# Moving 24 of 170 scatter columns from a graph kernel's first stage into its layers

## The chip, the core and the metric

The kernel runs on one core of one Trainium2 chip. A core has five engines with a queue each, which run in order and meet only at semaphores: TensorE (PE, matrix products), VectorE (DVE), ScalarE (ACT), GpSimd (POOL) and SyncE (SP, which mostly issues DMAs). The metric is device time in microseconds (us), the median of several runs; one execution was recorded by the profiler.

## What is computed

Three layers of a graph network over 1250 nodes of width 512 and 21,250 edges, then a residual norm, then a network over the edges with four attributes per edge, then the nodes again. Cut to what matters:

```
# first network, L = 3 layers
for l in range(3):
    neigh = segment_sum(h[src], dst) * inv_deg
    h = h @ Ws_self[l] + neigh @ Ws_neigh[l] + bs[l]      # relu but for the last
x = layernorm(x + h)
# second network
e     = mlp(edge_attr_4)                                   # 21250 x 4 -> 512
e_new = mlp([e, mesh_nfeat[src], x[dst]]) + e
agg   = segment_sum(e_new, dst)
x     = layernorm(x + mlp([x, agg]) + x)
```

## The kernel before

The edges are sorted by destination into 176 tiles of 128 edges, in ten buckets of 125 destination nodes each. The program has these stages.

*First stage* (`phase_a`). VectorE sorts and computes for each edge its slot. GpSimd writes the sorted index pairs to DRAM with 72 indirect DMAs (lines 400 and 404). An indirect DMA on GpSimd takes one column of up to 125 edges and sends each to the row that a table names; GpSimd generates its descriptors. The edge attributes, four floats per edge, go the same way into `s_attrs`, 170 columns (`EC`), one DMA each, by `scatter_attr` (line 145). `row_i` holds the rows, `k_attrs` the attributes. 24 of the columns (`ATTR_EARLY`) are issued in the first stage behind the pairs. Meanwhile TensorE makes weight products and the first layer's products. Last comes the *edge count*: for each tile VectorE makes two one-hot matrices (`hot_src`, line 605, and `hot_dst`, line 606), and TensorE multiplies them (lines 851 and 854) and adds them up into a table of edge counts by node pair, in three banks of PSUM. Four tiles are in flight; after four written out ones the loops run four tiles a pass. At the end of a bucket ScalarE copies the banks out. So that no tile is added before the copy of the bucket before, TensorE waits for a gate per tile and bank. SyncE opens the even tiles' gates and GpSimd the odd ones', both with the loop in `open_gates` (lines 272 to 277), which GpSimd reaches behind its 24 columns. The gates wait for `copied_out`, which TensorE starts at line 859.

*Graph layers* (`phase_b`). In each layer TensorE adds up the neighbours of ten groups of 125 nodes with the count table (lines 1226 and 1227, 20 matmuls a group, two groups ahead), VectorE mixes each sum with the node's own part (`b_mixed`, line 1052) and splits the table for the next (`b_a_lo`, line 1045), and then TensorE makes the next products (lines 73 to 75). GpSimd meanwhile issues `scatter(0, 130)`: the next 130 attribute columns, in batches of 17 (`BACKLOG`) with a semaphore for every second batch. Only in the third layer does somebody wait for GpSimd: VectorE's `normalise` handles two groups at a time, adds `x` (line 1060), takes mean and variance (lines 1063 to 1070), and GpSimd raises the variance to the power -1/2 (line 1015), which VectorE needs at line 1073. After every second power GpSimd issues four of the last 16 columns (`ATTR_LATE`), and after the last it loads the attributes back in slot order (line 1022).

*Edges and nodes* (`phase_c`, `phase_d`). About 1500 us of work on the edge tiles, where TensorE is nearly always busy, and then the nodes. GpSimd builds the operand from the attributes and gathers node rows.

Of the kernel before, what the change touches and what calls it, by code (L numbers as in the profile page):

```python
# [43 lines left out]
EP, EC = 125, E // 125  # L44
# [9 lines left out]
HALF_TILES = TILES // 2  # L54
PAD = P - 1
BACKLOG = 17
ATTR_EARLY, ATTR_LATE, ATTR_PAIR = 24, 16, 4
RECIP_BITS = 20
RECIP = (1 << RECIP_BITS) // NPB + 1
assert all(n * RECIP >> RECIP_BITS == n // NPB for n in range(N)) and N * RECIP < 1 << 24  # L60
# [77 lines left out]
def batched(columns, u):  # L138

    return sum(c // BACKLOG % 2 == u for c in range(columns))  # L140


def scatter_attr(pool, scratch, k, c):

    return pool.indirect_dma_start(scratch["attrs"], bass.IndirectOffsetOnAxis(ap=k["row_i"][0:EP, c:c + 1], axis=0),  # L145
                                   k["attrs"][0:EP, A4 * c:A4 * (c + 1)], None)
# [12 lines left out]
def phase_a(nc, ctx, t, scratch, keep):  # L159
# [9 lines left out]
    def sem(name):  # L169
        semaphores.append(nc.alloc_semaphore("a_" + name))  # L170
        return semaphores[-1]
# [60 lines left out]
    k, src_t, dst_t = keep, keep["src_t"], keep["dst_t"]  # L232
# [10 lines left out]
    count_bank, degree_bank = (bank[0], bank[1], bank[6]), bank[7]  # L243
    pairs_ok, attr_rows_ok = sem("pairs_ok"), sem("attr_rows_ok")
    scattered = [sem(f"scattered{i}") for i in range(2)]
    attr_scattered = [sem(f"attr_scattered{i}") for i in range(2)]
    pairs_in, pairs_read, pairs_turned = sem("pairs_in"), sem("pairs_read"), sem("pairs_turned")
    next_in = sem("next_in")
    centred, turned, turned_out, gains_ok, bias_mm, cols_ok = (
# [19 lines left out]
    def open_gates(engine, u):  # L269


        engine.wait_ge(tables_ok, 1)
        with engine.Fori(0, TILES // 2) as i:
            bucket1 = engine.value_load(k["tile_bucket1"][0:1, ds(2 * i + u, 1)], min_val=1, max_val=NB)
            for b in range(3):
                engine.wait_ge(copied_out[b], bucket1)
                engine.sem_inc(gate[b][u], 1)
# [8 lines left out]
    def rows_stored(u, upto):  # L286

        return 16 * (NJ // 2) + 16 * sum(len(names) for names, _, _ in vectors[u:upto:2])
# [83 lines left out]
    @block.gpsimd  # L372
    def _(pool):
        pool.iota(dst_grid[:], [[1, P]], base=0, channel_multiplier=0).then_inc(pool_const, 1)
        pool.iota(src_grid[:], [[NPB, NB], [1, P]], base=0, channel_multiplier=0).then_inc(pool_const, 1)
        pool.iota(tile_no[:], [[1, TILES + 1]], base=0, channel_multiplier=0,
                  allow_small_or_imprecise_dtypes=True).then_inc(pool_const, 1)
        pool.iota(k["grid"][:], [[1, P]], base=0, channel_multiplier=0,
                  allow_small_or_imprecise_dtypes=True).then_inc(pool_const, 1)
        pool.iota(place[:], [[-1, EC]], base=(1 << PLACE_BITS) - 1, channel_multiplier=0).then_inc(pool_const, 1)  # L380
        pool.iota(aside[:], [[1, EC]], base=SLOTS, channel_multiplier=ASIDE,
                  allow_small_or_imprecise_dtypes=True).then_inc(pool_const, 1)
        for i in range(2):
            pool.memset(jobs_out[i][:], 0.0).then_inc(pool_const, 1)
        pool.wait_ge(dve_const, 2)

        pool.affine_select(out=k["ident"][:], in_=k["ident"][:], compare_op=ALU.not_equal, fill=1.0, base=0,
                           pattern=[[-1, P]], channel_multiplier=1).then_inc(pool_const, 1)
        pool.affine_select(out=before[:], in_=before[:], compare_op=ALU.is_gt, fill=0.0, base=0,
                           pattern=[[1, P]], channel_multiplier=-1).then_inc(pool_const, 1)  # L390

        pool.wait_ge(pads_out, 32)
        pool.wait_ge(pairs_ok, 1)
        singles = scratch["pairs"].rearrange("a (b c) -> (a b) c", c=1)
        for c in range(CHUNKS + REST):
            u = c // BACKLOG % 2
            if c % BACKLOG == 0 and c >= 2 * BACKLOG:
                pool.wait_ge(scattered[u], 16 * batched(c, u))
            if c < CHUNKS:
                pool.indirect_dma_start(scratch["pairs"], bass.IndirectOffsetOnAxis(ap=chunk_row[:, c:c + 1], axis=0),  # L400
                                        sort_pay[:, CHUNK * c:CHUNK * (c + 1)].bitcast(F32), None).then_inc(scattered[u], 16)
            else:
                j, at = c - CHUNKS, c - CHUNKS + EC - REST
                pool.indirect_dma_start(singles, bass.IndirectOffsetOnAxis(ap=rest_row[:, j:j + 1], axis=0),
                                        sort_pay[:, at:at + 1].bitcast(F32), None).then_inc(scattered[u], 16)
        pool.wait_ge(attrs_in, 16)
        pool.wait_ge(attr_rows_ok, 1)
        for c in range(ATTR_EARLY):
            scatter_attr(pool, scratch, k, c).then_inc(attr_scattered[c // BACKLOG % 2], 16)
        open_gates(pool, 1)  # L410
        for u in range(2):
            pool.wait_ge(attr_scattered[u], 16 * batched(ATTR_EARLY, u))

    @block.vector
    def _(dve):
# [487 lines left out]
def phase_b(nc, ctx, t, scratch, keep):  # L903
# [9 lines left out]
    def sem(name):  # L913
        return ctx.enter_context(nc.semaphore("b_" + name))
# [3 lines left out]
    k = keep  # L918
# [27 lines left out]
    attr_scattered, attrs_in = [sem(f"attr_scattered{i}") for i in range(2)], sem("attrs_in")  # L946
# [19 lines left out]
    @block.sync  # L966
    def _(sp):
        for r in range(1, LAYERS):
            sp.wait_ge(w_split, 2 * r)
            for i in range(2):  # L970
                sp.dma_start(w[i][:], chunked(products[r][i])).then_inc(w_in, 16)
            sp.wait_ge(self_ok, NB * r)
            if r < LAST:
                sp.dma_start(bias[0][:], rows(t["L0_gnn_bs"][r + 1]).broadcast_to([P, D])).then_inc(bias_in, 16)
        sp.dma_start(bias[0][:], rows(t["L1_gnn_node_b0"]).broadcast_to([P, D])).then_inc(bias_in, 16)
        sp.dma_start(bias[1][:], rows(t["L1_gnn_edge_b0"]).broadcast_to([P, D])).then_inc(bias_in, 16)
        sp.dma_start(bias2[:], rows(scratch["edge_shift"]).broadcast_to([P, D])).then_inc(bias_in, 16)

        def load(i):
            if i >= X_BUFS:  # L980
                sp.wait_ge(res_ok, i - X_BUFS + 1)
            move_rows(sp, x[i % X_BUFS][:], node_rows(t["x"], node(LAST, i)), x_in[i % X_BUFS])

        for i in range(NB):
            load(i)
        edges.sync_first(sp)
        for i in range(NB):
            sp.wait_ge(u_lo_ok, NB * LAST + i + 1)
            u = i % OUT_BUFS
            if i < HEAD:  # L990
                move_rows(sp, node_rows(scratch["dst_head"], i), out[u][:, 1, :], head_stored[i])
            move_rows(sp, node_rows(scratch["node_own"], i), out[u][:, 0, :], stored[u])
            move_rows(sp, node_rows(scratch["dst_table"], i), out[u][:, 1, :], stored[u])
            edges.sync_early(sp, i)
        for i in range(NB):
            move_rows(sp, node_rows(scratch["x1"], i), h[:, i, :], x1_stored)
        for u in range(OUT_BUFS):
            sp.wait_ge(stored[u], 2 * MOVED * len(range(u, NB, OUT_BUFS)))
        edges.sync(sp)

    @block.gpsimd
    def _(pool):
        def scatter(first, end):
            for c in range(first, end):
                u = c // BACKLOG % 2
                if c % BACKLOG == 0 and c >= 2 * BACKLOG:
                    pool.wait_ge(attr_scattered[u], 16 * batched(c, u))
                scatter_attr(pool, scratch, k, ATTR_EARLY + c).then_inc(attr_scattered[u], 16)

        columns = EC - ATTR_EARLY  # L1010
        scatter(0, columns - ATTR_LATE)
        for i in range(NB):
            pool.wait_ge(var_ok, i + 1)
            pool.sem_inc(tick, 1)
            pool.tensor_tensor(dev[i % 2][:, 1:2], dev[i % 2][:, 0:1], k["half"][0:NPB, :], ALU.pow).then_inc(dev_ok, 1)
            left = ATTR_LATE - ATTR_PAIR * (i // 2)
            if i % 2 and left > 0:
                scatter(columns - left, columns - left + ATTR_PAIR)
                if left == ATTR_PAIR:
                    for u in range(2):  # L1020
                        pool.wait_ge(attr_scattered[u], 16 * batched(columns, u))
                    pool.dma_start(k["attrs"][:], scratch["attrs"].rearrange("(p t) a -> p (t a)", p=P)).then_inc(attrs_in, 16)
        pool.wait_ge(attrs_in, 16)
        edges.gpsimd(pool)
# [1236 lines left out]
```

## Time and profile before

| | us |
|---|---|
| median of 3 runs | 2257.26 |
| lowest and highest | 2256.71, 2258.75 |
| the profiled execution's own time | 2256.75 |
| its span in the trace | 2255.0 |
| first stage, to the start of the layers | 324 |
| graph layers | 324 to about 640 |

Busy over the span: TensorE 97%, VectorE 67%, ScalarE 54%, GpSimd 54%. A timeline row gives the start, the duration, the engine, the line, the operation with output and inputs, a count where equal neighbours are merged, and in brackets the idle time of the engine before it with what ended it. "POOLq" and the like are the sequencers of the engines, which read the queue, wait and branch ahead of the engine proper.

### The profile page before, as it was taken

The numbers are of one execution on the slowest core, as the hardware profiler recorded it, in microseconds if no ns is written. First come the engines' busy times: TensorE is split into PE (matmuls) and PEld (weight loads), VectorE is DVE, ScalarE is ACT, GpSimd is POOL, SyncE is SP. The second block draws the span as 40 slices with busy tenths as digits, with TensorE's granted clock in tenths as the row PEclk, the third lists the DMA queues.
The fourth block names the chain that finished last, engine by engine and source line by source line (L and its number), as shares of the span: only waits on it lengthen the run. The fifth ranks groups of instructions, "written<-read, shape, count | busy, mean of one in ns | idle before, by whom it ended". The sixth has DMA issues, their size and how long they took to land. (4 is left out here: it accounts for less than half of the span.)

```text
span 2255.0 us, 44895 instructions
## 1 busy us (share of the span) xinstructions
PE 2190.3 (97%) x13039; PEld 1881.9 (83%) x13040; DVE 1502.7 (67%) x3372; ACT 1218.0 (54%) x2244; POOL 1206.8 (54%) x1721
## 2 busy tenths in 40 slices
PE   7999989999999999999999999999999999999898
PEld 4367888888789989899898998989989989889776
DVE  8425975344756777767767667766776676767666
ACT  2221114333256676677666767667667667667421
POOL 0775028885535555565555555555555555555223
PEclk9999999999999999999999999999999999999899
DMA  6421001112363333323332333333323332333131
GB/s 203 127 56 41 0 6 40 8 40 54 114 210 88 64 62 63 62 60 65 60 65 61 65 60 65 63 63 60 65 60 60 65 65 61 60 65 65 27 92 44
DMA packets 81814, 149.81 MB, mean 66 GB/s; under 512 B 20523, under 2 KB 20989, under 8 KB 81754
## 3 DMA queue, kind: packets, MB, share of 16 engines
q0 software_dynamic: 47248, 93.38, 21.5%
q1 hardware_dynamic: 34505, 55.67, 7.8%
q8 instruction: 33, 0.54, 0.1%
q14 instruction: 28, 0.22, 0.0%
HBM read 128.90 MB, written 19.71 MB: 66 GB/s over the span
## 5 line engine op out<-in xcount | busy, mean ns | idle before, releaser
L1667 ACT ACTIVATE b_bank<-c_bias 128x512 f32<-128x512 f32 x528 | 316.4, 599 | 15.1 <-PE b_bank L1779 10.0
L145 POOL DMA_INDIRECT s_attrs<-k_attrs,k_row_i x170 | 224.4, 1320 | 168.0 <-POOLq L2233 117.2
L1600 DVE CUSTOM_DVE_ANT_0 b_bank<-b_bank,c_p,k_floor 128x512 f32<-128x512 f32 x176 | 132.5, 753 | 255.5 <-PE b_bank L1801 254.6
L1445 POOL DMA_INDIRECT c_from_src<-s_dst_table,c_at_nodes x173 | 278.5, 1610 | 32.2 <-issue 32.2
L1856 PE MATMUL b_bank<-k_m_hi,c_pt_hi 128*128 128x512 f32 x704 | 293.8, 417 | 0.0
L1432 POOL DMA_INDIRECT c_from_src<-s_mesh_table,c_at_nodes x176 | 202.3, 1149 | 152.3 <-POOL c_at_nodes L1428 142.5
L1857 PE MATMUL b_bank<-k_m_lo,c_pt_hi 128*128 128x512 f32 x704 | 277.9, 395 | 0.0
L1451 POOL TENSOR_TENSOR c_dev<-c_var,k_half 128x1 f32<-128x1 f32 x176 | 99.3, 564 | 327.5 <-DVE c_var L1582 327.5
L1858 PE MATMUL b_bank<-k_m_hi,c_pt_lo 128*128 128x512 f32 x704 | 273.9, 389 | 0.0
L1738 ACT ACTIVATE c_h<-c_from_src 128x512 f32<-128x512 f32 x176 | 111.3, 632 | 263.4 <-DVE c_from_src L1621 263.4
L1799 PE MATMUL b_bank<-c_m_hi,c_ht_hi 128*128 128x384 f32 x704 | 222.5, 316 | 6.3 <-DVE c_ht_lo L1587 6.0
L1799 PE MATMUL b_bank<-k_m_hi,c_pt_hi 128*128 128x384 f32 x704 | 224.7, 319 | 0.0
L1801 PE MATMUL b_bank<-c_m_hi,c_ht_lo 128*128 128x384 f32 x704 | 218.6, 311 | 0.0
L1800 PE MATMUL b_bank<-c_m_lo,c_ht_hi 128*128 128x384 f32 x704 | 217.7, 309 | 0.0
L1801 PE MATMUL b_bank<-k_m_hi,c_pt_lo 128*128 128x384 f32 x704 | 217.1, 308 | 0.0
L1800 PE MATMUL b_bank<-k_m_lo,c_pt_hi 128*128 128x384 f32 x704 | 216.9, 308 | 0.0
L1616 DVE SCALAR_TENSOR_TENSOR c_rp_lo<-c_p,c_dev,c_rp_hi 128x512 fp32r<-128x512 f32 x176 | 132.3, 751 | 74.0 <-ACT c_rp_hi L1730 73.8
L1858 PEld LDWEIGHTS b_bank<-k_m_hi,c_pt_lo 128*128 128x128 f32 x704 | 132.8, 189 | 32.4
L1730 ACT ACTIVATE c_rp_hi<-c_p,c_dev 128x512 fp32r<-128x512 f32 x176 | 127.7, 726 | 54.9 <-POOL c_dev L1467 54.9
L1663 ACT ACTIVATE c_p<-b_bank 128x512 f32<-128x512 f32 x176 | 105.6, 600 | 92.3 <-PE b_bank L1776 91.7
L1467 POOL TENSOR_TENSOR c_dev<-c_var,k_half 128x1 f32<-128x1 f32 x176 | 133.0, 756 | 40.5 <-DVE c_var L1603 35.9
L1856 PEld LDWEIGHTS b_bank<-k_m_hi,c_pt_hi 128*128 128x128 f32 x704 | 132.4, 188 | 23.9
(352 smaller groups left out, 5859.9 us busy)
## 6 DMA issues: line engine op xcount, KB each, us to landing
c_from_src<-s_mesh_table,c_at_nodes POOLq DMA_INDIRECT x176
c_from_src<-s_dst_table,c_at_nodes POOLq DMA_INDIRECT x173, 4.7
s_attrs<-k_attrs,k_row_i POOLq DMA_INDIRECT x170
a_mesh<-in_L_gnn_mesh_nfeat_dram SPq DMA_DIRECT2D x10, 224.0 KB
k_h<-in_x_dram SPq DMA_DIRECT2D x10, 224.0 KB
s_mesh_table<-a_mesh_out SPq DMA_DIRECT2D x10, 224.0 KB
b_x<-in_x_dram SPq DMA_DIRECT2D x10, 224.0 KB
s_node_own<-b_out SPq DMA_DIRECT2D x10, 224.0 KB
```

The lines of the kernel that those rows point to most:

```text
L145: return pool.indirect_dma_start(scratch["attrs"], bass.IndirectOffsetOnAxis(ap=k["row_i"][0:EP, c:c + 1], axis=0), k["attrs"][0:EP, A4 * ...
L1432: pool.indirect_dma_start(from_src[u][:], None, scratch["mesh_table"], bass.IndirectOffsetOnAxis(ap=at_nodes[u][:, 0:1], axis=0)).then_inc ...
L1445: pool.indirect_dma_start(from_src[u][:], None, scratch["dst_head" if head else "dst_table"], bass.IndirectOffsetOnAxis(ap=at_nodes[u][:, ...
L1467: pool.tensor_tensor(dev[u][:, 0:1], var[u][:, 2:3], k["half"][:], ALU.pow).then_inc(dev1_ok, 1)
L1600: dve.tensor_tensor_reduce(var1_bank[:], var1_bank[:], p[u % 2][:], 1.0 / D, k["floor"][:, 0:1], ALU.mult, ALU.add, var[u][:, 0:1]).then_i ...
L1667: act.activation(bank[:], bias[:, m, :], ACT.Copy).then_inc(bank_set, 1)
L1799: pe.matmul(to, left[0][:, c, :], high, start=False, stop=False, skip_group_check=True)
L1800: pe.matmul(to, left[0][:, c, :], low, start=False, stop=False, skip_group_check=True)
L1801: last = pe.matmul(to, left[1][:, c, :], high, start=False, stop=(c == KC - 1), skip_group_check=True)
L1856: pe.matmul(edge_bank[:], left[0], m_hi[1][:, c, :], start=False, stop=False, skip_group_check=True)
L1857: pe.matmul(edge_bank[:], left[0], m_lo[1][:, c, :], start=False, stop=False, skip_group_check=True)
L1858: last = pe.matmul(edge_bank[:], left[1], m_hi[1][:, c, :], start=False, stop=(c == KC - 1), skip_group_check=True)
```

## The change

The constant for the early columns is gone. All 154 columns that were not among the last 16 are issued at the start of the layers, where 130 were; the first stage issues none. The wait for the 24 at the end of the first stage and its two semaphores go too, and the semaphores of the layers count from column 0.

```diff
-ATTR_EARLY, ATTR_LATE, ATTR_PAIR = 24, 16, 4
+ATTR_LATE, ATTR_PAIR = 16, 4
...
         pool.wait_ge(attrs_in, 16)
         pool.wait_ge(attr_rows_ok, 1)
-        for c in range(ATTR_EARLY):
-            scatter_attr(pool, scratch, k, c).then_inc(attr_scattered[c // BACKLOG % 2], 16)
         open_gates(pool, 1)
-        for u in range(2):
-            pool.wait_ge(attr_scattered[u], 16 * batched(ATTR_EARLY, u))
...
-                scatter_attr(pool, scratch, k, ATTR_EARLY + c).then_inc(attr_scattered[u], 16)
-
-        columns = EC - ATTR_EARLY
-        scatter(0, columns - ATTR_LATE)
+                scatter_attr(pool, scratch, k, c).then_inc(attr_scattered[u], 16)
+
+        scatter(0, EC - ATTR_LATE)
         for i in range(NB):
...
             if i % 2 and left > 0:
-                scatter(columns - left, columns - left + ATTR_PAIR)
+                scatter(EC - left, EC - left + ATTR_PAIR)
```

GpSimd's queue at the end of the first stage, before: the last pair DMAs, the 24 attribute columns, the gate loop (the table's entry is loaded at L274), the end of the stage, and the first instruction of the layers.

```order
18 L404 DMA s_pairs<-a_sort_pay,a_rest_row 44700x1 x30
19 L145 DMA s_attrs<-k_attrs,k_row_i 22528x4 x24
20 L273 UNCONDITIONAL_BRANCH
21 L273 ISA
22 L274 TENSOR_LOAD k_tile_bucket
23 L274 ISA x2
24 L273 REGISTER_ALU
25 L273 COMPARE_AND_BRANCH
```

The same place after the change (line numbers are up to six lower):

```order
18 L403 DMA s_pairs<-a_sort_pay,a_rest_row 44700x1 x30
19 L272 UNCONDITIONAL_BRANCH
20 L272 ISA
21 L273 TENSOR_LOAD k_tile_bucket
22 L273 ISA x2
23 L272 REGISTER_ALU
24 L272 COMPARE_AND_BRANCH
```

The gate loop now stands directly behind the pairs.

GpSimd's queue from the start of the layers to the second pair of powers, before:

```order
28 L1001 UNCONDITIONAL_BRANCH
29 L145 DMA s_attrs<-k_attrs,k_row_i 22528x4 x130
30 L1015 TENSOR_TENSOR b_dev_2164<-b_dev_2164,k_half 125x1
31 L1015 TENSOR_TENSOR b_dev_2165<-b_dev_2165,k_half 125x1
32 L145 DMA s_attrs<-k_attrs,k_row_i 22528x4 x4
```

The same place after it:

```order
27 L996 UNCONDITIONAL_BRANCH
28 L145 DMA s_attrs<-k_attrs,k_row_i 22528x4 x154
29 L1009 TENSOR_TENSOR b_dev_2138<-b_dev_2138,k_half 125x1
30 L1009 TENSOR_TENSOR b_dev_2139<-b_dev_2139,k_half 125x1
31 L145 DMA s_attrs<-k_attrs,k_row_i 22528x4 x4
```

24 more columns stand ahead of the first two powers; the groups of four behind them are as before. The queues of the other engines keep their order.

## Rows read from the trace of the kernel before

**Rows 1.** Timeline of GpSimd, first and last early column, first column of the layers.
```profile
171.83 1.19 POOL L145 DMA_INDIRECT s_attrs<-k_attrs,k_row_i  x1 [0.30 <-issue]
...
206.17 1.18 POOL L145 DMA_INDIRECT s_attrs<-k_attrs,k_row_i  x1 [0.30 <-issue]
...
324.53 1.19 POOL L145 DMA_INDIRECT s_attrs<-k_attrs,k_row_i  x1 [117.17 <-POOLq L2233]
```

**Rows 2.** Stretches: length, busy us (instructions) per engine, granted clock, DMA share, GB/s.
```profile
195.00:200.00 5.00, 5.00 (x49) 3.86 (x48) 3.24 (x8) 0.60 (x1) 4.00 (x4) 1.00 0.09 5
200.00:205.00 5.00, 2.31 (x25) 1.39 (x22) 1.09 (x3) 0.00 (x0) 3.87 (x4) 0.94 0.09 4
205.00:210.00 5.00, 3.21 (x26) 2.40 (x27) 2.71 (x9) 0.00 (x0) 2.05 (x2) 0.50 0.07 2
```

**Rows 3.** Timeline of VectorE, one-hot tiles in the loop's first passes.
```profile
200.17 0.57 DVE L605 TENSOR_SCALAR a_hot_src<-a_src_grid,k_src_t 128x1280 bf16<-128x1280 int16 x1 [1.32 <-PE a_bank L854]
...
204.65 0.57 DVE L605 TENSOR_SCALAR a_hot_src<-a_src_grid,k_src_t 128x1280 bf16<-128x1280 int16 x1 [3.75 <-remote]
...
207.66 0.55 DVE L605 TENSOR_SCALAR a_hot_src<-a_src_grid,k_src_t 128x1280 bf16<-128x1280 int16 x1 [2.29 <-remote]
...
208.30 0.55 DVE L605 TENSOR_SCALAR a_hot_src<-a_src_grid,k_src_t 128x1280 bf16<-128x1280 int16 x1
...
211.05 0.55 DVE L605 TENSOR_SCALAR a_hot_src<-a_src_grid,k_src_t 128x1280 bf16<-128x1280 int16 x1 [0.17 <-PE a_bank L854]
```

**Rows 4.** Timeline of TensorE, count matmuls of tile 0 and of tile 4.
```profile
198.76 0.17 PE L854 MATMUL a_bank<-a_ones,a_hot_dst 128*128 128x2 bf16 x1
...
202.28 0.23 PE L851 MATMUL a_bank<-a_hot_dst,a_hot_src 128*128 128x128 bf16 x1 [0.45 <-issue]
202.99 0.27 PE L851 MATMUL a_bank<-a_hot_dst,a_hot_src 128*128 128x128 bf16 x2 [0.48 <-issue]
```

**Rows 5.** Sequencers by line: count, ns min/median/max, first and last start us.
```profile
L273 POOLq MOVE  x1: 29/29/29, 189.5 to 189.5; - x1
...
L859 PEldq EVENT_SEMAPHORE  x3: 51/51/51, 194.7 to 195.0; - x3
...
L274 POOLq SEQ_ASSERT  x1: 590/590/590, 205.3 to 205.3; - x1
```

**Rows 6.** Timeline of GpSimd, last column before the powers, first and second powers.
```profile
532.80 1.19 POOL L145 DMA_INDIRECT s_attrs<-k_attrs,k_row_i  x1 [0.30 <-issue]
553.72 1.20 POOL L1015 TENSOR_TENSOR b_dev<-b_dev,k_half 125x1 f32<-125x1 f32 x2 [19.73 <-DVE b_dev L1070]
...
564.78 1.19 POOL L1015 TENSOR_TENSOR b_dev<-b_dev,k_half 125x1 f32<-125x1 f32 x2 [1.89 <-DVE b_dev L1070]
```

**Rows 7.** Timeline in the second layer, a column of GpSimd and VectorE beside it.
```profile
439.47 2.19 POOL L145 DMA_INDIRECT s_attrs<-k_attrs,k_row_i  x1 [0.30 <-issue]
...
439.11 1.48 DVE L1045 TENSOR_TENSOR b_a_lo<-k_adj,b_a_hi 125x1280 fp32r<-125x1280 int16 x1
```

**Rows 8.** Timeline of VectorE in the third layer, around the first pair.
```profile
550.68 1.28 DVE L1060 TENSOR_TENSOR b_mixed<-b_mixed,b_x 125x512 f32<-125x512 f32 x2
...
554.33 1.18 DVE L1073 TENSOR_SCALAR k_h<-b_mixed,b_moments,b_dev 125x512 f32<-125x512 f32 x2 [0.65 <-POOL b_dev L1015]
555.43 0.74 DVE L1052 SCALAR_TENSOR_TENSOR b_mixed<-b_bank,b_inv_degree,k_h 125x512 f32<-125x512 f32 x1
```

**Rows 9.** Stretches, columns as in rows 2, in the third layer.
```profile
555.00:560.00 5.00, 5.00 (x24) 4.14 (x23) 5.00 (x5) 2.32 (x2) 4.34 (x3) 1.00 0.05 1
```

**Rows 10.** Timeline of TensorE, first matmul of the seventh sum (sum 6).
```profile
567.36 0.47 PE L1226 MATMUL b_bank<-b_u_hi,b_a_hi 125*128 125x512 f32 x1 [0.65 <-DVE b_mixed L1052]
```

**Rows 11.** Timeline of TensorE, large matmuls after its idle time at 320.
```profile
325.08 0.80 PE L1226 MATMUL b_bank<-b_u_hi,b_a_hi 125*128 125x512 f32 x1 [4.55 <-ACT b_a_hi L1153]
...
330.75 0.40 PE L1226 MATMUL b_bank<-b_u_hi,b_a_hi 125*128 125x512 f32 x1
330.98 0.40 PE L1227 MATMUL b_bank<-b_u_lo,b_a_hi 125*128 125x512 f32 x1
```

**Rows 12.** Timeline of VectorE, the last pair.
```profile
595.41 1.16 DVE L1073 TENSOR_SCALAR k_h<-b_mixed,b_moments,b_dev 125x512 f32<-125x512 f32 x2 [2.15 <-POOL b_dev L1015]
```

More of the change, by code:

```diff
@@ L245, in phase_a @@
     scattered = [sem(f"scattered{i}") for i in range(2)]
-    attr_scattered = [sem(f"attr_scattered{i}") for i in range(2)]
     pairs_in, pairs_read, pairs_turned = sem("pairs_in"), sem("pairs_read"), sem("pairs_turned")
@@ L1017, in _ @@
             if i % 2 and left > 0:
-                scatter(columns - left, columns - left + ATTR_PAIR)
+                scatter(EC - left, EC - left + ATTR_PAIR)
                 if left == ATTR_PAIR:
                     for u in range(2):
-                        pool.wait_ge(attr_scattered[u], 16 * batched(columns, u))
+                        pool.wait_ge(attr_scattered[u], 16 * batched(EC, u))
                     pool.dma_start(k["attrs"][:], scratch["attrs"].rearrange("(p t) a -> p (t a)", p=P)).then_inc(attrs_in, 16)
```

## The prediction

> **What bounds the kernel now.** The change only moves GpSimd's descriptor work, so I read GpSimd's own timeline first, then whoever waits at the two places from which and to which the work moves. [Rows 1] is GpSimd's timeline: the 24 early columns start at 171.83 us and the last at 206.17, one every 1.49 us (34.34 / 23), each 1.19 busy and 0.30 idle. Then GpSimd issues nothing more until the graph layers start at 324.53.
>
> The first place is the edge count, which begins at about 198 us. The table by stretches [rows 2] shows TensorE 5.00 of 5.00 us busy until 200, then 2.31 and 3.21 of 5.00, and the granted clock at 0.50 in the second of these. VectorE's timeline [rows 3] says how much is lost: it makes the one-hot tiles, and from 207.66 to 208.30 it makes one in 0.64 us, the pace that it keeps to the end of the count. But the first tiles of its loop start at 200.17, 204.65, 207.66 and 208.30, after idle times of 1.32, 3.75 and 2.29 us, the last two put down to nothing that the profile can name ("remote"). TensorE trickles in the same way: two matmuls, then 0.45 to 0.48 us of "issue" [rows 4]. The gates are not the cause: GpSimd's sequencer had entered the gate loop at 189.5, ahead of its own queued columns, and the gates were held only by TensorE's start signal at 194.7; yet that sequencer too shows a register check of 590 ns at 205.3 [rows 5]. All sequencers slow together, the pieces come one every 0.71 to 0.76 us, half of GpSimd's 1.49, and it ends at 207.4, when the last early column ends (206.17 + 1.18). I read it as contention between the descriptor work of the columns and four engines that all issue small instructions at their highest rate; the trace shows the coincidence and not the mechanism.
>
> The second place is the last graph layer. GpSimd's timeline [rows 6]: the 130th layer column starts at 532.80 and ends at 533.99, and then GpSimd waits 19.73 us for the first variances (b_dev, line 1070), which arrive at 553.72. That is all the room there is: 553.72 - 534.29 = 19.4 us before the first power on line 1015 is late.
>
> **What the change does, part by part.**
>
> *Out of the first stage: 24 columns, 24 x 1.49 = 35.8 us of GpSimd and 24 scatters.* GpSimd was not waited for there directly. What goes is the overlap with the start of the count. Three tiles after 200.17 at 0.64 is 202.1; the same tile started at 208.30 [rows 3]: 6.2 us. The 1.32 us before 200.17 would mostly go as well (tile 0 had been counted by 198.93 [rows 4]), up to 0.9, and the 0.17 and similar idle times near 211, which follow from the clock at 0.50, up to 0.5. So the gain is 6.2 to 7.6 if my reading is right and 0 if it is wrong; I take **-7.0**. It passes on whole, since the rest of the count runs at VectorE's pace and what follows starts when the count has ended. The waits for the scatter's semaphores at the stage's end go too, at nothing: those scatters had landed 110 us earlier.
>
> *Into the layers: the same 24 columns ahead of the first power.* They stand in GpSimd's queue before line 1015, and nothing can overtake them. In the old clock of the layers (all of it moves by the gain above), columns 131 to 154 start at 534.29 and, at 1.49 each, end at 570.1. Some are dearer: a column that starts while VectorE runs a two-input operation waits for that operation's end. The one at 439.47 took 2.19 us instead of 1.19 while a_lo ran from 439.11 to 440.59 [rows 7], so it was held 1.0. Between 540 and 552 there are three a_lo of 1.48 us and the two adds of the first pair, the last of them in [rows 8]; laying the columns on them one after another gives 0.4 + 1.0 + 1.3, with some rounding 2.4 us. Bounds: 0 (no column meets one) and 5.6 (three times 1.48 and 1.2 in full). So GpSimd comes free at 572.5, against 553.72: the first pair's power is **18.8 us late** (16.4 to 21).
>
> The Trainium skill ("SBUF — State Buffer", section "Who interferes with whom") infers that a tensor_tensor does not hold up descriptor generation. The row at 439.47 speaks against it here; by the page the 2.4 would be 0, the lateness 16.4 and the total 2.4 lower.
>
> *What of the 18.8 reaches the end.* VectorE waits at line 1073 for that power (0.65 us now), and everything behind it on VectorE is in order: the two normalised tiles, the next mix at 555.43, the next a_lo [rows 8]. From 555 to 560 VectorE is busy 5.00 of 5.00 us [rows 9], and it is so to 593.3 (595.41 - 2.15 [rows 12]) except 0.6 us for each power and small gaps: it has no slack in which to catch up. TensorE has hardly any either: it runs two sums ahead and already waits 0.65 us for b_mixed at 567.36 [rows 10]; so it passes the delay on whole. It would stand still for some 17 us from 557.5 and restart at a low clock. After the 4.55 us gap at 325.08 it ran at half speed till 330.75: 12 of the large matmuls at 0.43 us instead of 0.23 [rows 11], 2.5 us lost. Here that is hidden: sum 4 would end at 556.1 + 18.8 + 4.5 + 2.5 = 581.9, and VectorE asks for it only at 566.47 + 18.8 = 585.3. If this cover were gone it would cost 2.5; I take 0. The waits that follow keep their size: GpSimd has four late columns between two powers as before, and the 2.15 us before 595.41 [rows 12] hangs on GpSimd's own chain, which is shifted like the rest. The reload of the attributes behind the last column moves along with it, with no new waiter. From 601 on TensorE has the lead again, and the edges run as before. So **+18.8**.
>
> *Small things.* GpSimd's queue is 24 entries longer in one place and shorter in another; SyncE's queue is unchanged. The removed semaphores and the renumbered batches cost nothing: the first batch wait in the layers comes 34 columns in, when 17 have long landed.
>
> **Sum.** 2256.75 (the profiled run's own time; its span is 2255.0) - 7.0 + 18.8 = 2268.55. The median of the runs shown is 2257.26, 0.5 above, which is within their spread; I state **2268.8**.
>
> **Rivals.**
> 1. *The count starts no sooner.* The stall at 200 to 208 belongs to something else that stays, such as the first pass through the loops' code. For it: it starts as VectorE and TensorE enter their loops at 200, and later bucket ends have no such stall. Against: GpSimd's sequencer had been in its loop since 189.5 and stalls as well, the half-period of 0.74 us is GpSimd's, and the stall ends with the last column. Gain 0: 2256.75 + 18.8 = 2275.6. The Trainium skill ("Runtime: NRT & Kernel Launch", "Instruction fetch mechanics") says that a taken branch outside the pages at hand forces a fetch before execution goes on. By that rule the stall would stay, which is this rival; VectorE's long idle times however stand inside the straight code of one pass, which speaks against it.
> 2. *The lateness costs more than itself.* GpSimd stays behind after the first pair, since the late columns meet other VectorE operations, or the low clock is not covered. Each group of four has little slack (GpSimd waited 1.89 us before the power at 564.78 [rows 6]); if a group takes 1 us more than its slack, or the 2.5 us of clock shows, the sum is 3 to 6 higher: 2272 to 2275.
> 3. *Faster than before.* The lateness is absorbed in the last layer, because TensorE and VectorE there have work that can go ahead of line 1073, so only the gain is left: 2256.75 - 7.0 = 2249.8. It decides once less than 7 of the 18.8 us gets through. Against it: VectorE's queue is in order, it has nothing but that wait, and TensorE already waits for it at 567.36 [rows 10]. Even columns at 1.19 without the idle 0.30 would be late by 8.9 (534.0 + 24 x 1.19 - 553.72).
>
> **How the numbers follow.** Chances: the forecast 0.74 (its own range 2265 to 2271.5: gain 6.2 to 7.6, lateness 16.4 to 21), rival 1 0.13, rival 2 0.08, rival 3 0.05. The likeliest is the forecast, 2268.8. To hold 8 times in 10 the range must take in part of rivals 1 and 2: 2265 to 2276. A measurement of this kernel can tell about 0.2% (4.5 us) from no change. Faster by more than that: 0.04; within: 0.04 (a mostly absorbed delay); slower: 0.92.
>
> **What would show it.** Right: VectorE's loop tiles follow each other at 0.64 us from 200 on and the granted clock stays at 1.00 there; the layers start at about 317.5 instead of 324.5; the first power follows directly on a column, at about 565.5 on the new clock; VectorE idles about 19 us before line 1073 once, and TensorE about 17 before a sum; later waits are as before. Rival 1: the same idle times of 3.75 and 2.29 at the loop's start. Rival 2: longer VectorE waits for the second to fourth powers. Rival 3: no long VectorE idle time at line 1073. The forecast would be wrong above all if columns ran at another pace than 1.49 us in the stretch from 534 on.

## The result and the profile after

The changed kernel took 2268.88 us (median of 5 runs, 2264.41 to 2271.16) against 2257.26 before (5 runs, 2256.71 to 2258.75). The ratio is 1.0041, with a 95% interval from 1.0029 to 1.0052: slower by 6.5 to 11.7 us. (The ratio isn't the quotient of the two medians, which lie 11.6 us apart, at the upper end of that interval.) The profiled execution was the shortest of the five, 2264.41 us, with a span of 2262.7.

**The first place.** Stretches of the kernel after, columns as in [rows 2]:

```profile
200.00:205.00 5.00, 5.00 (x97) 5.00 (x95) 4.99 (x17) 0.00 (x0) 0.00 (x0) 1.00 0.00 2
205.00:210.00 5.00, 4.50 (x79) 4.10 (x77) 5.00 (x17) 1.43 (x4) 0.00 (x0) 1.00 0.00 0
```

VectorE's timeline after, the first tiles of its loop:

```profile
199.50 0.55 DVE L600 TENSOR_SCALAR a_hot_src<-a_src_grid,k_src_t 128x1280 bf16<-128x1280 int16 x1 [0.25 <-PE a_bank L849]
200.23 0.55 DVE L600 TENSOR_SCALAR a_hot_src<-a_src_grid,k_src_t 128x1280 bf16<-128x1280 int16 x1
200.86 0.55 DVE L600 TENSOR_SCALAR a_hot_src<-a_src_grid,k_src_t 128x1280 bf16<-128x1280 int16 x1
```

TensorE does 97 matmuls in the stretch from 200, where it did 25 [rows 2]; the granted clock stays at 1.00; the tiles come every 0.63 us; and the waits of 1.32, 3.75 and 2.29 us [rows 3] are one of 0.25 us. GpSimd's timeline after, from the last pair to the layers, and at the end of the long row of columns:

```profile
170.81 1.19 POOL L403 DMA_INDIRECT s_pairs<-a_sort_pay,a_rest_row  x1 [0.30 <-issue]
317.28 1.18 POOL L145 DMA_INDIRECT s_attrs<-k_attrs,k_row_i  x1 [145.28 <-POOLq L2227]
...
561.75 1.18 POOL L145 DMA_INDIRECT s_attrs<-k_attrs,k_row_i  x1 [0.30 <-issue]
562.95 1.21 POOL L1009 TENSOR_TENSOR b_dev<-b_dev,k_half 125x1 f32<-125x1 f32 x2
...
574.02 1.19 POOL L1009 TENSOR_TENSOR b_dev<-b_dev,k_half 125x1 f32<-125x1 f32 x2 [1.90 <-DVE b_dev L1064]
```

The layers start at 317.28 instead of 324.53. The wait of 19.73 us before the first power [rows 6] is gone; the power stands directly behind a column. The second power has its wait of 1.90 us, as before.

**The second place.** VectorE's timeline after: the instruction for the first pair's variances, the first pair, the last pair.

```profile
545.12 0.27 DVE L1064 TENSOR_SCALAR b_dev<-b_moments 125x1 f32<-125x1 f32 x2
563.59 1.16 DVE L1067 TENSOR_SCALAR k_h<-b_mixed,b_moments,b_dev 125x512 f32<-125x512 f32 x2 [18.20 <-POOL b_dev L1009]
...
605.01 1.16 DVE L1067 TENSOR_SCALAR k_h<-b_mixed,b_moments,b_dev 125x512 f32<-125x512 f32 x2 [2.51 <-POOL b_dev L1009]
```

TensorE's timeline and the stretches around it:

```profile
565.55 0.76 PE L1220 MATMUL b_bank<-b_u_hi,b_a_hi 125*128 125x512 f32 x1 [16.20 <-DVE b_mixed L1046]
...
570.38 0.40 PE L1221 MATMUL b_bank<-b_u_lo,b_a_hi 125*128 125x512 f32 x1
```
```profile
555.00:560.00 5.00, 0.00 (x0) 0.00 (x0) 0.00 (x0) 0.00 (x0) 4.04 (x4) 0.50 0.08 2
...
565.00:570.00 5.00, 4.45 (x11) 3.51 (x12) 5.00 (x5) 3.07 (x2) 4.39 (x3) 0.50 0.05 1
570.00:575.00 5.00, 5.00 (x23) 4.09 (x22) 4.30 (x10) 1.28 (x1) 2.80 (x4) 0.96 0.37 104
```

From 555 to 560 TensorE, VectorE and ScalarE do nothing and GpSimd issues columns. VectorE waits 18.20 us where it waited 0.65 [rows 8], and TensorE 16.20 us. TensorE then runs at half speed till 570.4, while VectorE beside it is busy 5.00 of 5.00 us, so this low clock is hidden: the second power comes 11.07 us after the first (574.02 - 562.95), against 11.06 before.

**Where the time went.** Measured from marks in the two traces:

| piece, us | before | after | difference |
|---|---|---|---|
| first tile of VectorE's count loop at | 200.17 | 199.50 | -0.67 |
| from it to the layers' first column | 124.36 | 117.78 | -6.58 |
| from there to the first power | 229.19 | 245.67 | +16.48 |
| the rest of the span | 1701.28 | 1699.75 | -1.53 |
| span | 2255.0 | 2262.7 | +7.7 |

The third row is the lateness, the second the gain. The first and the last differ from run to run of the same kernel: a second trace of the changed kernel (below) starts its loop at 202.33 and spans 2266.9.

### The profile page after: what moved, and what is told of

It reads as the page before. It is cut to its first block and busy times, and to the rows that moved or that the text cites. A ratio compares the mean times of both kernels' runs of the same rounds, so it can differ in the third digit from the quotient of the medians.

```text
span 2262.7 us, 44890 instructions
## 1 busy us (share of the span) xinstructions
PE 2186.2 (97%) x13036; PEld 1879.4 (83%) x13040; DVE 1501.2 (66%) x3372; ACT 1218.3 (54%) x2244; POOL 1209.3 (53%) x1721
```

## The experiments

Theory A, the one on record: columns issued on GpSimd at the start of the edge count slow all engines there while they last (cost about 7), and 24 more columns ahead of the first power make it late by about 18.8, which passes on whole. Rivals: the slow start has another cause that stays; the layers' end absorbs part; GpSimd's delay grows behind the first pair. The kernels of each of the four rounds ran on one chip beside the kernel before.

**The changed kernel again**, on the chip of the next three.

> The changed kernel once more, for a second profile and for its spread: its runs lay between 2264.4 and 2271.2, those of before within 2 us. Forecast: median about 2268.5; the layers start at 317 and VectorE waits 18.2 us in each profile, so that what differs between runs lies later or in the clock.

Measured: 2268.64 us against 2258.12, ratio 1.0053 (1.0039 to 1.0067). Its distances are 117.78 from the loop's first tile to the layers and 245.68 from there to the first power, within 0.01 of the first trace. So both terms repeat, and what varies is the start of the count and the part behind the layers. The layers start at 320.11 in this trace, not at the expected 317, because the count starts 2.8 us later.

**The 24 columns left out altogether.** The kernel leaves out part of the attribute table, so its result is not that of the task; the time shows the gain without the price.

```diff
+ATTR_LATE, ATTR_PAIR = 16, 4          # none early
...
-        scatter(0, columns - ATTR_LATE)
+        scatter(0, EC - ATTR_LATE - 24)
```

> The changed kernel with 24 of its 170 attribute columns left out, those of the layers just ahead of the last 16: the first stage is as in the changed kernel, the layers have 130 columns ahead of the first power as before the change. Only the gain is left. Forecast (contention of the columns with the start of the edge count): 2257.3 - 7.0 = 2250.3, layers start at about 317, VectorE waits 0.6 us for the first power. Rival 1 (the stall belongs to the loops' first pass): 2257 and layers at 324.

Measured: 2251.81 us, ratio 0.9970 (0.9959 to 0.9981), that is -6.8 us (-9.3 to -4.3). The distance from loop to layers is 117.76, and GpSimd waits for the first variances again (the layers start at 321.30, not at 317, since the loop's first tile comes as late as 203.54):

```profile
549.50 1.20 POOL L1009 TENSOR_TENSOR b_dev<-b_dev,k_half 125x1 f32<-125x1 f32 x2 [18.25 <-DVE b_dev L1064]
```

**The 24 columns twice**: early as before, and once more ahead of the first power.

```diff
+        for c in range(24):
+            scatter_attr(pool, scratch, k, c).then_inc(repeated, 16)
         for i in range(NB):
```

> The kernel before, with the 24 early columns issued a second time in the layers behind the 130, ahead of the first power (the same values to the same rows). Only the lateness is left. Forecast: GpSimd is free 18 to 19 us late and all of it reaches the end: 2257.3 + 18.8 = 2276, layers start at 324.5. If part of the lateness were absorbed downstream: under 2272. If the low clock after TensorE's idle time showed as well: about 2278.

Measured: 2274.46 us, ratio 1.0073 (1.0060 to 1.0087), +16.5 us (13.5 to 19.6). VectorE's timeline of this kernel shows the stall of the first place and the wait of the second, side by side:

```profile
206.38 0.76 DVE L605 TENSOR_SCALAR a_hot_src<-a_src_grid,k_src_t 128x1280 bf16<-128x1280 int16 x1 [3.58 <-remote]
...
572.71 1.17 DVE L1076 TENSOR_SCALAR k_h<-b_mixed,b_moments,b_dev 125x512 f32<-125x512 f32 x2 [16.72 <-POOL b_dev L1017]
```

The first power comes 245.67 us after the layers' start, as in the changed kernel. The two halves add up: -6.8 + 16.5 = +9.7, between the 9.3 and the 12.0 that the two ratios of the changed kernel give. Within intervals this wide, no absorption and no growth. The traces say it more sharply. From the first power to the end, the four kernels in which that power is late (the changed one twice, this one, and the one with eight early columns below) take 1699.75 to 1703.84 us, 1701.6 on average; the other ten traces take 1700.60 to 1702.90, and 1701.6 on average too.

**Sixteen early columns.** The eight that overlapped the count go to the layers, where there is room for them.

```diff
-ATTR_EARLY, ATTR_LATE, ATTR_PAIR = 24, 16, 4
+ATTR_EARLY, ATTR_LATE, ATTR_PAIR = 16, 16, 4
```

> The kernel before with 16 early columns instead of 24, so 138 ahead of the first power in the layers. The last early column ends at about 195.5, ahead of the count's start at 198, and the layers' columns end at about 547, ahead of the first variances at 553.7. Forecast: the whole gain and no lateness, 2257.3 - 7.2 = 2250. Rival 1: 2257.

Measured: 2251.48 us, ratio 0.9971 (0.9962 to 0.9981), that is -6.5 us. It beats both kernels. GpSimd's last early column, VectorE's first loop tile, and the first power:

```profile
195.22 1.19 POOL L145 DMA_INDIRECT s_attrs<-k_attrs,k_row_i  x1 [0.30 <-issue]
```
```profile
201.38 0.55 DVE L606 TENSOR_SCALAR a_hot_src<-a_src_grid,k_src_t 128x1280 bf16<-128x1280 int16 x1 [0.25 <-PE a_bank L855]
```
```profile
547.57 1.20 POOL L1016 TENSOR_TENSOR b_dev<-b_dev,k_half 125x1 f32<-125x1 f32 x2 [6.43 <-DVE b_dev L1071]
```

The loop's code is the same as before; only the columns beside it are gone, and so is the stall. That refutes rival 1 as it was put.

**Twenty, and eight early columns** (the same constant at 20 and at 8).

> Twenty columns stay in the first stage and 134 go into the layers. Contention theory (descriptor work of the columns slows every sequencer at the count's start, only while it lasts): the last early column ends about 6 us earlier than with 24, one or two microseconds after VectorE enters the count's loop, so one short stall of 0.5 to 1.5 us is left at the loop's start instead of 6.2, the granted clock stays at 1.00 or nearly, and GpSimd still waits some 12 us for the first variances. Time 5 to 6 us below before: about 2252.5. Theory that the stall is all or nothing (it takes any overlap at all to put TensorE to its low clock and cost the 6 us): about 2257, with TensorE at 0.50 for some microseconds. If columns had no part in it: as before.

Measured: 2252.68 us against 2258.91, ratio 0.9968 (0.9956 to 0.9980). In this trace the last early column ran from 201.16 to 202.35 and VectorE's loop began at 202.79, so there was no overlap, no stall, and the distance to the layers was 117.28. The run doesn't show what a small overlap costs. It does show that columns beside the four tiles written out ahead of the loop cost little: one tile takes 0.81 us instead of 0.55.

```profile
198.82 0.81 DVE L606 TENSOR_SCALAR a_hot_src<-a_src_grid,k_src_t 128x1280 bf16<-128x1280 int16 x1
```

> Eight columns stay in the first stage and 146 go into the layers, the last 16 as before. In the layers 154 columns made the first power 16.5 us late; at 1.54 us a column eight fewer make it 16.5 - 12.3 = 4.2 us late. Theory that lateness passes on whole: GpSimd waits 0 for the first variances, VectorE waits about 4.5 to 5 us for the first power, TensorE stands still for 2 to 4 us, and the time is the 2251.5 of the kernel with 16 early columns plus 4.2: 2255 to 2256.5. Theory that the layers' end can absorb a small delay (VectorE or TensorE has slack of a few microseconds there): 2251.5 to 2253.

Measured: 2257.70 us, ratio 0.9993 (0.9984 to 1.0002). GpSimd, VectorE and TensorE:

```profile
552.66 1.21 POOL L1016 TENSOR_TENSOR b_dev<-b_dev,k_half 125x1 f32<-125x1 f32 x2
```
```profile
553.30 1.16 DVE L1074 TENSOR_SCALAR k_h<-b_mixed,b_moments,b_dev 125x512 f32<-125x512 f32 x2 [6.27 <-POOL b_dev L1016]
```
```profile
555.26 0.76 PE L1227 MATMUL b_bank<-b_u_hi,b_a_hi 125*128 125x512 f32 x1 [4.27 <-DVE b_mixed L1053]
```

VectorE waits 5.6 us longer than its usual 0.65, and the ratio is 0.0022, or 5.0 us, above that of 16 early columns (on another chip), and 0.0025, or 5.6 us, above that of 20 early columns on this one. As far as intervals of 2 to 3 us on each side can tell, a delay of 5 us passes on whole too. I had expected 4.2, and the miss was mine: in the changed kernel VectorE's own extra wait is 18.20 - 0.65 = 17.55, since the variances are ready 1.0 us sooner there, and 17.55 less eight times 1.49 is 5.6. Eight early columns are the break-even.

**What about a column stalls the count?** Two kernels with 16 early columns and another load beside the loop. In the first, ScalarE issues ten plain DMAs of 125 pieces of 16 bytes each:

```diff
         act.wait_ge(tables_ok, 1)
+        for c in range(10):
+            act.dma_start(scratch["aside"][c * EP:(c + 1) * EP, :], k["attrs"][0:EP, A4 * c:A4 * (c + 1)]).then_inc(aside_out, 16)
```

> Sixteen early columns as in the faster kernel, and beside them ten plain DMAs of 125 pieces of 16 bytes each, issued by ScalarE at the start of the edge count into a scratch tensor that nothing reads. They move what ten columns move, in pieces of the same size, but the descriptors don't come from GpSimd. If it is GpSimd's descriptor work that slows the sequencers: no stall, VectorE's loop tiles 0.62 to 0.64 apart, time 2251.5 as without them (ScalarE has room). If it is the traffic of small pieces, or the queues' bookkeeping: a stall of some microseconds at the loop's start and 2254 to 2258.

Measured: 2252.84 us, ratio 0.9966 (0.9953 to 0.9980). In the stretch from 205 on the DMA share is 0.10, more than the 0.07 of [rows 2], and nothing is slowed (117.68 us from the loop's first tile to the layers):

```profile
205.00:210.00 5.00, 5.00 (x99) 5.00 (x96) 4.99 (x17) 0.00 (x0) 0.00 (x0) 1.00 0.10 4
```

In the second, GpSimd does eight powers without a DMA:

```diff
+        for i in range(8):
+            pool.tensor_tensor(busy[:, 8 * i:8 * i + 8], busy[:, 80:88], busy[:, 88:96], ALU.pow)
         open_gates(pool, 1)
```

> Sixteen early columns as in the faster kernel, and behind them eight powers on GpSimd of 128x8 elements each, with no DMA, ahead of its gates. GpSimd is then busy at the count's start but generates no descriptors. If a busy GpSimd as such (its memory accesses) is what slows the others: a stall at the loop's start for as long as the powers run, 2253 to 2258. If it takes descriptor work: no stall and 2251.5. A power of 8 elements a partition is expected to take 0.6 to 1.2 us; should they end before the loop starts, the run tells nothing.

Measured: 2251.71 us, ratio 0.9965 (0.9952 to 0.9979). The loop's first tile starts at 203.14 and the layers 117.58 us later. GpSimd's row, and the stretch in which it was busy all the time:

```profile
196.70 14.11 POOL L413 TENSOR_TENSOR a_busy<-a_busy 128x8 f32<-128x8 f32 x8
```
```profile
205.00:210.00 5.00, 5.00 (x98) 5.00 (x96) 5.00 (x17) 0.00 (x0) 5.00 (x4) 1.00 0.00 0
```

So neither small transfers that ScalarE issues nor a GpSimd busy with arithmetic slows the count. What is left of a column is the indirect DMA as GpSimd issues it.

**Twenty-eight and thirty-two early columns**: more overlap.

> Twenty-eight early columns, four more than before, 126 in the layers. The columns then overlap the edge count's loop for 6 us longer than before (to about 213). Contention theory: the stall lasts until the last early column ends, and 7.2 us of overlap cost 6.2 before, so 6 us more cost about 5: VectorE's tiles stand 2 to 4 us apart until about 213, the layers start 5 us later relative to the loop's first tile than before (129 instead of 124.4), time about 2263. Theory that the stall belongs to the loop's start alone and needs only any overlap there: no more than before, 2258. GpSimd enters its gates later by 6 us (195.5); a wait for a gate on TensorE would be seen and would stand for itself.

> Thirty-two early columns, eight more than before, 122 in the layers. Contention theory: 12 us more of overlap, 10 more of stall, time about 2268, VectorE's tiles far apart and the clock at 0.50 until about 219. Loop's start alone: 2258. GpSimd's sequencer reaches the gates 12 us later than before (about 201), which could hold the tiles from the second on by up to 3 us whatever the theory.

Measured: 2263.04 us, ratio 1.0021 (1.0011 to 1.0030), and 2264.73 us, ratio 1.0026 (1.0014 to 1.0037), against 2257.95. With 28, VectorE's tiles and GpSimd's last early column:

```profile
207.48 0.57 DVE L606 TENSOR_SCALAR a_hot_src<-a_src_grid,k_src_t 128x1280 bf16<-128x1280 int16 x1 [3.74 <-remote]
211.20 0.78 DVE L606 TENSOR_SCALAR a_hot_src<-a_src_grid,k_src_t 128x1280 bf16<-128x1280 int16 x1 [2.99 <-remote]
213.41 0.55 DVE L606 TENSOR_SCALAR a_hot_src<-a_src_grid,k_src_t 128x1280 bf16<-128x1280 int16 x1 [1.26 <-remote]
```
```profile
213.51 1.60 POOL L145 DMA_INDIRECT s_attrs<-k_attrs,k_row_i  x1 [0.30 <-issue]
```

With 32, a stretch 10 us behind the loop's start, and the last early column:

```profile
215.00:220.00 5.00, 3.36 (x28) 2.73 (x28) 2.87 (x7) 0.00 (x0) 3.62 (x4) 0.50 0.08 2
```
```profile
218.33 1.21 POOL L145 DMA_INDIRECT s_attrs<-k_attrs,k_row_i  x1 [0.30 <-issue]
```

TensorE's rows of the same kernel, from the first pass of the loop (tile 6) and from its second pass (tile 8):

```profile
215.85 0.48 PE L852 MATMUL a_bank<-a_hot_dst,a_hot_src 128*128 128x128 bf16 x3 [0.33 <-issue]
218.63 1.24 PE L852 MATMUL a_bank<-a_hot_dst,a_hot_src 128*128 128x128 bf16 x10 [0.36 <-DVE a_hot_dst L607]
```

More columns make the stall longer, but it doesn't last quite to their end. TensorE's trickle of one to three matmuls per 0.74 us ends at 211.2 with 28 columns and at 216.1 with 32, and VectorE's last wait put down to "remote" ends at 213.41 and 216.00, while the last column ends at 215.11 and 219.54. Behind that TensorE makes a tile's ten matmuls in one go, in about 1.25 us, which is its pace at the low clock. In all four stalled traces the trickle begins at the entry into the loops (at the earliest with the last matmul of the last tile written out) and ends within their first pass (tiles 4 to 7), and with 32 columns the second pass has columns beside it and no trickle. So a third reading is left, that the stall takes both, columns and the first pass through the loops' code. No run here has all its columns behind the first pass, which would tell the two apart.

The expected direction holds; the size was overdone (2263 was met, 2268 was not). GpSimd's gates, which it opens later in these two kernels, don't explain the loss: within the columns' time TensorE's rows name such a gate once, for 0.47 us at 207.31 with 28 columns, and not at all with 32.

Over the traces so far, with the overlap counted from VectorE's first loop tile to the end of the last early column, and the loss against 117.7, the distance without one:

| early columns | overlap, us | loop to layers, us | loss, us |
|---|---|---|---|
| 0 to 20 | 0 | 117.3 to 117.8 | 0 |
| 24 (the doubled kernel) | 6.5 | 124.5 | 6.8 |
| 24 (before) | 7.2 | 124.4 | 6.7 |
| 28 | 12.1 | 127.1 | 9.4 |
| 32 | 15.4 | 130.7 | 13.0 |

Are instruction fetches the reason? The DMA view of 205 to 220 of the kernel with 32 columns lists one packet of an instruction queue in these 15 us, most of which are stall (queue, kind: packets, MB, share):

```profile
q14 instruction: 1, 0.01, 0.2%
```

The window 185 to 215 of the kernel before and that of the kernel after have two such packets each, one on q8 and one on q14. The Trainium skill ("Runtime: NRT & Kernel Launch", "Instruction fetch mechanics") says that a taken branch to a page not at hand forces a fetch by DMA; with one packet in fifteen microseconds, repeated fetches are not what the engines wait for here.

**Are the loops needed?** The kernel before, with its 24 early columns, but twelve tiles written out ahead of the loops instead of four: on both engines (VectorE in the same way), then on TensorE alone (shown).

```diff
-        with pe.Fori(1, GROUPS) as i:
+        for n in range(GROUP, 3 * GROUP):
+            count(n, n % GROUP, True)
+        with pe.Fori(3, GROUPS) as i:
```

> The kernel before with its 24 early columns, but VectorE and TensorE have twelve tiles of the edge count written out ahead of their loops, not four; the same instructions otherwise. The last early column ends at about 207.5. If the stall needs only columns beside instructions at a high rate: it starts at about 200 and lasts to 207.5 as before, 6.2 us lost, 2258. If it needs the loops (what a taken branch costs, while GpSimd generates descriptors): the eight more tiles pass at 0.64 us each, to about 205.5, and only 1 to 2 us are lost: 2253 to 2254.

> As the kernel before, but only TensorE has twelve tiles written out; VectorE enters its loop after four as before. If the stall needs TensorE's own loop: its matmuls keep coming ten in 0.58 us as soon as their tile is there, and VectorE loses little, 2253 to 2255. If VectorE's loop is enough (or all instruction streams are slowed whatever they are): TensorE's matmuls trickle, two in 0.74 us, inside straight code, 2258.

Measured: 2251.98 us and 2251.84 us. That is what the expectation for "the loops are needed" says, but on the chip of this round the kernel before itself took 2252.71 us (21 runs, 2249.42 to 2255.20), 5 to 6 less than in the other rounds, and the ratios are 0.9998 (0.9989 to 1.0007) and 0.9997 (0.9988 to 1.0006). So the comparison tells nothing of the loops. What the trace of the second of them does show is an overlap without a stall. VectorE's loop began at 201.53, here are tiles of it, a column beside them and the stretch:

```profile
206.01 0.54 DVE L605 TENSOR_SCALAR a_hot_src<-a_src_grid,k_src_t 128x1280 bf16<-128x1280 int16 x1
206.63 0.75 DVE L605 TENSOR_SCALAR a_hot_src<-a_src_grid,k_src_t 128x1280 bf16<-128x1280 int16 x1
207.50 0.54 DVE L605 TENSOR_SCALAR a_hot_src<-a_src_grid,k_src_t 128x1280 bf16<-128x1280 int16 x1
```
```profile
207.36 1.19 POOL L145 DMA_INDIRECT s_attrs<-k_attrs,k_row_i  x1 [0.30 <-issue]
```
```profile
200.00:205.00 5.00, 5.00 (x87) 4.65 (x85) 4.75 (x12) 0.56 (x1) 4.08 (x4) 1.00 0.12 7
```

Every second tile takes 0.75 us instead of 0.54, and 7.0 us of overlap cost 0.7 (118.41 to the layers against 117.7). The other trace, in which VectorE's tiles from the fifth to the twelfth are written out too, is alike: 6.9 us of overlap counted from the fifth tile, and 118.26 to the layers. One longer tile beside a column is also what the tiles ahead of the loop show on the other chips (above), so this small cost is common to all and the stall comes on top of it. The chip isn't faster as such: both kernels take what the unstalled ones took elsewhere (2251.5 to 2252.8), and from the first power to the end they need 1700.96 and 1701.92 us, against 1701.28 in the kernel before. I therefore think that the kernel before doesn't stall on this chip; its own trace there wasn't taken, so this rests on its time alone.

## Why the prediction was right

The forecast was its likeliest case: 2268.55 from the sum, 2268.88 measured, and each mechanism was found where it was put. That the two numbers agree to 0.3 us is luck. The traces of before and after put the two terms at -7.3 and +16.5 (the first two rows of the table of pieces, and the third), 2.6 us less in all than the forecast's -7.0 and +18.8; what makes up for it is that the changed kernel's runs spread over 7 us and their median lies 4.5 us above the profiled run.

- *Gain, -7.0.* The traces give -6.6 from the loop's first tile on, and the wait ahead of it went from 1.32 to 0.25, another 1.1: 7.65 in all, at the upper of the bounds of 6.2 and 7.6. The run without the columns gives -6.8. The reading of [rows 3] and [rows 5], one stall that ends with the last column, was right for this kernel; its explanation was too wide. The "four engines that all issue small instructions at their highest rate" are not stalled by such columns wherever they meet: the tiles written out ahead of the loops lose some 0.2 us and those in the two traces of the last round 0.2 us on every second one, and neither stalls.
- *Lateness, +18.8.* Measured 16.5, at the lower bound. Three sizes were off. First, the last column's trailing idle of 0.30 was counted, but the power follows directly (0.3). Second, the 131st column starts 208.8 us after the layers' start (526.06 - 317.28), not 209.8 as in the old trace (1.0): over the first 130 columns the holds add up to 14.6 us after and 15.7 before, since VectorE's operations come about 1 us sooner against the columns (the last point of this document says why). Third, the columns were held by 1.35 us in place of 2.4 (1.0, rounded): 0.30, 1.00 and 0.05. (The prediction's own three, 0.4 + 1.0 + 1.3, make 2.7 and not 2.4, and with the bound of 5.6 its upper end would be 22 and not 21. Neither slip matters beside the measured 1.35 and 16.5.) I had let the adds of the first pair hold a column like an operation of their own. The traces show the rule (the last section): those adds start just as a_lo ends, and the column that waited for a_lo slips through.
- *What reaches the end.* All of it, as forecast. The doubled kernel costs 16.5 us for 16.5 us of lateness, and the kernel with eight early columns 5.0 to 5.6 for 5.6. The low clock was hidden, as worked out from [rows 11]. The later waits stayed (1.90 against 1.89 [rows 6]; 2.51 against 2.15 [rows 12]).
- *The rivals.* Rival 1 (no gain) is refuted by the trace after and by sixteen early columns; that the loops' first pass is a second condition beside the columns, as the kernels with 28 and 32 suggest, is not. Rival 2 (lateness costs more) would need longer waits at the later powers, and none grew by more than 0.4 us. Rival 3 (absorbed) would need no wait on VectorE at the first power, where there are 18.20 us.
- *The Trainium skill's rule.* At [rows 7] the trace spoke against the inference of the Trainium skill ("SBUF — State Buffer", "Who interferes with whom") that a tensor_tensor doesn't hold up descriptor generation, and the trace after does so again. That inference would have given a lateness of 16.4, nearer to 16.5 than mine, for a wrong reason: 1.35 us of holds are there, and the two other errors above, of 0.3 and 1.0, nearly cancel them.

*Open:* whether the stall needs the loops' first pass besides the columns, and why a column stalls four engines in one trace and takes 0.2 us from every second tile in another. In the stalled traces TensorE advances one to three matmuls every 0.74 us, half of the columns' 1.49, so an event that comes twice per column may set the pace; which one, no run here shows. Nor is the chip proven to be what decides: the two traces from the last chip are of kernels with other code than the stalled ones, and single runs stray on the same chip too (of the seven with 32 early columns one took 2258.88 us, the others 2262.55 to 2267.64).

## What to carry to other kernels

Filling an engine's idle time pays only up to the moment at which somebody waits for that engine: 19.4 us of room took some 13 columns, and each of the other 11 cost its 1.49 us in full, because it stood in an in-order queue ahead of the one small instruction that the whole layer waits for. When moving work, ask for the amount at each place, not all or nothing: of the 24 columns 16 were free where they were and 8 free where they went, and that split gave the gain (0.9971) without the price. A gain that comes from a stall between engines should be measured on more than one chip, since here the stall itself seems to depend on it. On the chip of the last round the gain would be about 0.7 us by the two traces there, and this change would cost some 16 us; that is an estimate from 16.5 less 0.7, and no run there measured it.

## What the runs showed of the hardware

- *VectorE's operations with both inputs in SBUF hold a column until they end.* In the kernel after, GpSimd's and VectorE's timelines around 541:

```profile
536.82 2.19 POOL L145 DMA_INDIRECT s_attrs<-k_attrs,k_row_i  x1 [0.30 <-issue]
...
542.29 1.24 POOL L145 DMA_INDIRECT s_attrs<-k_attrs,k_row_i  x1 [0.30 <-issue]
```
```profile
536.46 1.48 DVE L1039 TENSOR_TENSOR b_a_lo<-k_adj,b_a_hi 125x1280 fp32r<-125x1280 int16 x1
...
540.99 1.48 DVE L1039 TENSOR_TENSOR b_a_lo<-k_adj,b_a_hi 125x1280 fp32r<-125x1280 int16 x1
542.39 1.28 DVE L1054 TENSOR_TENSOR b_mixed<-b_mixed,b_x 125x512 f32<-125x512 f32 x2
```

  The column at 536.82 ends at 539.01, which is 1.07 us after a_lo ends (537.94). The one at 542.29 ends at 543.53, 1.06 after the second a_lo (542.47), although the adds run from 542.39 to 543.67. So a held column ends 1.06 us after the operation that was running when it started, and one that starts later, even without a gap, doesn't hold it again. An add alone does hold: in each of the 14 traces the column that starts 0.8 us into the last pair's adds takes 1.56 us instead of 1.19. Operations of VectorE that read one input from a PSUM bank (`b_bank`) don't hold: in the layers of the 14 traces 427 columns start beside one (`b_mixed` at line 1052, and `b_u_lo`, `k_h` and `b_ht_lo` from the bank), and all took 1.18 to 1.24 us.
- *The stall at the count's start* costs, where it comes, 0.8 to 1.05 us for each us of overlap with GpSimd's indirect DMAs. Ten plain DMAs of the same piece size (share 0.10) and 14.11 us of GpSimd arithmetic cost nothing. The trickle of matmuls was seen at the entry into the loops and in their first pass alone.
- *The low clock at the layers' start differs.* TensorE, idle for 4.55 us at 325.08 before, ran at half speed for 5.7 us [rows 11]; after, idle for 4.72 us, it did so for 3.5:

```profile
317.84 0.80 PE L1220 MATMUL b_bank<-b_u_hi,b_a_hi 125*128 125x512 f32 x1 [4.72 <-ACT b_a_hi L1147]
...
321.32 0.39 PE L1221 MATMUL b_bank<-b_u_lo,b_a_hi 125*128 125x512 f32 x1
```

  With that, VectorE's instruction for the first variances starts 227.84 us after the layers, instead of 228.88. The other traces bear the link out. Where TensorE restarts at half speed for 3.5 us (also the second trace of the changed kernel, and eight early columns), it starts at 227.84 to 227.87; for 4.4 us (16 and 32 early columns), at 228.25 to 228.28; for 6.6 us (the doubled kernel, and 28), at 229.30 to 229.36. So each further us at half speed costs about half a us. The idle time before it doesn't sort them: it was 4.50 us with eight early columns and 4.51 in the doubled kernel. It brought the changed kernel nothing, since there the columns decide.
